# A relational graph network on one core: one gathered tile in 66, and two in 66 in the last layer, are loaded row by row from other queues than GpSimd's

## The reference

```python
h = relu(layernorm(x))
x = x + segment_sum((h * src_norm)[src], dst) * dst_norm      # layer 0
h = relu(layernorm(x))
for l in range(2):                                            # layers 1 and 2
    seg = dst * 65 + edge_type
    agg = segment_sum(h[src], seg)
    cnt = maximum(segment_sum(1, seg), 1)
    conv = relu(einsum('nrd,rdk->nk', agg / cnt, W[l]) + h @ root[l] + bias[l])
    h = conv + relu(h @ res_W[l] + res_b[l])
out = x + h
```

## Time and profile before

| | |
|---|---|
| median of 3 runs | 12882.89 us (12865.02 to 12885.59) |
| the profiled execution | 12863.82 us, its span 12861.9 us |
| POOL | busy 9338.7 us (73%) |
| PE | busy 5821.2 us (45%) |
| DVE | busy 5213.0 us (41%) |
| ACT | busy 1786.2 us (14%) |
| mean granted TensorE clock | 0.693 of 2.4 GHz |

### The profile page before, as it was taken

How to read it: one execution, slowest core, us unless ns; L and a number is a source line. 1 busy time by engine, 2 the same in 40 slices (tenths; PEclk the granted TensorE clock), 3 DMA queues, 4 the chain that set the end, 5 groups by cost and what they waited for, 6 DMA issues and landing times.

```text
span 12861.9 us, 134064 instructions
## 1 busy us (share of the span) xinstructions
PE 5821.2 (45%) x30566; PEld 4624.6 (36%) x30766; DVE 5213.0 (41%) x19303; ACT 1786.2 (14%) x4595; POOL 9338.7 (73%) x9756
## 2 busy tenths in 40 slices
PE   3544444444444445555555555554333333333333
PEld 3433333333333334333333333333333333333333
DVE  9866666666666642222222222222222222222222
ACT  5611111111111111111111111110000000000000
POOL 3277777777777767777777777776777777777776
PEclk6777777777777777777777777776666666666666
DMA  1244444444444442222222222222111111111112
GB/s 42 51 143 140 142 140 145 138 145 138 145 139 144 138 113 78 83 82 80 79 81 83 82 81 78 83 83 52 28 28 28 28 28 28 28 28 28 28 28 36
DMA packets 523546, 1050.43 MB, mean 82 GB/s; under 512 B 216706, under 2 KB 249232, under 8 KB 523280
## 3 DMA queue, kind: packets, MB, share of 16 engines
q1 hardware_dynamic: 212816, 729.64, 15.5%
q0 software_dynamic: 310464, 318.54, 13.2%
HBM read 600.17 MB, written 447.31 MB: 81 GB/s over the span
## 4 chain that ended last, share of the span: by engine, by line
POOL 69%; issue 26%; DVE 2%; DMA 1%; PE 1%; POOLq 1%; SPq 0%; DVEq 0%; ACT 0%; ACTq 0%
POOL rows L518 69%; DVE ystage L885 2%; DMA rows<-h_table,idx_st 1%; PE sums_ps L787 0%; POOLq L512 0%; POOLq L261 0%; DMA rows<-y_table,idx_st 0%; SPq L290 0%; DMA y_table<-ystage 0%; DVEq L879 0%; POOLq L260 0%; DMA h_table<-scr 0%; PE y_ps L738 0%; DVEq L885 0%; SPq L270 0%
## 5 line engine op out<-in xcount | busy, mean ns | idle before, releaser
L518 POOL DMA_INDIRECT rows<-y_table,idx_st x6468 | 6133.4, 948 | 2075.7 <-issue 2075.7
L787 PE MATMUL sums_ps<-onehot,rows 128*64 128x128 f32 (+1 forms) x19404 | 3896.8, 390 | 6487.1 <-DMA rows<-y_table,idx_st 4459.9
L787 PEld LDWEIGHTS sums_ps<-onehot,rows 128*64 128x64 f32 (+1 forms) x19404 | 3645.0, 211 | 6705.9 <-issue 5114.4
L518 POOL DMA_INDIRECT rows<-h_table,idx_st x3234 | 3083.7, 954 | 1010.3 <-issue 1005.7
L914 DVE TENSOR_SCALAR onehot<-iota,dst_rel,w_sb 128x128 f32<-128x128 bf16 x6468 | 1727.7, 361 | 3986.2 <-PE sums_ps L749 2276.9
L921 DVE TENSOR_SCALAR_CACHE_REDUCE w_raw<-scr,key_col 128x384 bf16<-128x384 f32 x3234 | 1744.6, 603 | 0.0
L738 PE MATMUL y_ps<-w_parts,hT 128*128 128x512 bf16 (+1 forms) x5200 | 1256.4, 375 | 194.0 <-ACT hT L614 161.0
L912 DVE TENSOR_SCALAR onehot<-iota,dst_rel 128x128 f32<-128x128 bf16 x3234 | 676.3, 300 | 1105.9 <-PE sums_ps L749 899.5
L601 ACT ACTIVATE idx_st<-pair_i 128x11 int32 (+1 forms) x594 | 125.9, 213 | 7162.6 <-PE sums_ps L787 4875.4
L622 ACT ACTIVATE ystage<-y_ps 128x512 f32<-128x512 f32 (+1 forms) x1800 | 1020.8, 567 | 517.8 <-PE y_ps L738 411.8
L984 DVE TENSOR_SCALAR rr<-rr 128x64 f32<-128x64 f32 x200 | 43.4, 217 | 2145.6 <-PE block_ps L759 2145.6
(11 more groups left out here) (125 smaller groups left out, 1759.1 us busy)
## 6 DMA issues: line engine op xcount, KB each, us to landing
y_table<-ystage SPq DMA_DIRECT2D x400, 768.0 KB, 3.6
scr<-key_row SPq DMA_DIRECT2D x297, 832.0 KB, 7.3
y_table<-ystage SPq DMA_DIRECT2D x200, 608.0 KB, 3.1
rows<-y_table,idx_st POOLq DMA_INDIRECT x6468, 2.4
rows<-h_table,idx_st POOLq DMA_INDIRECT x3234
rr<-y_table SPq DMA_DIRECT2D x200, 64.0 KB, 1.8
w_raw<-in_L_gnn_W SPq DMA_DIRECT2D x4, 1040.0 KB
h_table<-scr SPq DMA_DIRECT2D x1, 3200.0 KB, 17.0
```

The lines of the kernel that those rows point to most:

```text
L518: pool.indirect_dma_start(out=rows[:, j, k, 0:D], out_offset=None, in_=table, in_offset=bass.IndirectOffsetOnAxis(ap=idx_st[:, j, k:k + 1] ...
L787: ins = nc.tensor.matmul(sums_ps[u][0:width, c:c + P], rows[:, j, k, 0:width], onehot[:, (J * u + j) % 2, k, :], start=False, stop=False)
```

## The change

In every pair of steps the last tile of the last group, (u, j, k) = (1, 2, 10), is no longer gathered by POOL. SP loads its 128 rows with 128 DMAs of one row each, into a buffer of its own, `rows_sp`. For that it reads the row numbers into 32 registers at a time from a new table in HBM (`idx_row`), in four parts of 32 rows: parts 0 and 2 at the start of steps u = 0 and u = 1, parts 1 and 3 between the second and the third save. It may begin when PE is through with the pair before. In layer 2 the last tile of group (0, 2) goes the same way through ACT's queue into `rows_act`: parts 2 and 3 behind the staging at j = 1 of step 0, and parts 0 and 1 of the next pair behind the stagings at j = 1 and j = 2 of step 1. PE waits for these rows before the group that holds the tile. POOL's loop now has a body of two steps. The prologue gets two conversions on DVE, which make the row numbers, and two DMAs that save them.

```diff
+            for k in range(2):
+                sp.wait_ge(idx_ready, k + 1)
+                sp.dma_start(idx_row[k].rearrange("(c p) e -> p c e", p=P),
+                             i_row[k].rearrange("p (c e) -> p c e", e=P)).then_inc(idx_saved, 16)
...
+            def load_rows(l, i, part):
+                table = h0_table if l == 0 else y_table[l - 1]
+                tile_of = (i * 2 + 1) * T + T - 1
+                sp.load(row_regs, idx_row[min(l, 1)][bass.ds(tile_of, 1), part * PART:(part + 1) * PART])
+                for n, reg in enumerate(row_regs):
+                    e = part * PART + n
+                    at = sp.snap(reg, min_val=0, max_val=table.shape[0] - 1)
+                    sp.dma_start(rows_sp[e:e + 1, 0:D], table[bass.ds(at, 1), :])\
+                      .then_inc(row_loaded[l][part], 16)
...
                     with sp.Fori(0, S // 2) as i:
+                        wait_alone(sp, agg_done[l], i * 2 * J + J)
                         for u in range(2):
                             s = i * 2 + u
+                            load_rows(l, i, 2 * u)
...
                                 save_y(l, s, u, range(YG - 1))
+                            load_rows(l, i, 2 * u + 1)
...
-                            for k in range(K):
+                            for k in range(K - 1 if (u, j) == (1, J - 1) or (l, u, j) == (2, 0, J - 1) else K):
                                 pool.indirect_dma_start(
...
                                 stage(l, s + 1, j)
                                 if l < 2:
                                     emit_y(l, s, u, i, Y_AFTER[j])
+                                elif u == 0 and j == 1:
+                                    load_rows(i, 2)
+                                    load_rows(i, 3)
+                                elif u == 1:
+                                    load_rows(i + 1, j - 1)
...
+                                if (l, u, j) == (2, 0, J - 1):
+                                    for half in range(2):
+                                        pe.wait_ge(row_loaded_act[half], (i + 1) * (32 * PART))
+                                if (u, j) == (1, J - 1):
+                                    for part in range(4):
+                                        pe.wait_ge(row_loaded[l][part], (i + 1) * 16 * PART)
...
             dve.wait_ge(tr_done, TG)
+            dve.wait_ge(tr_done, 2 * TG)
+            dve.wait_ge(win_ready, 1)
+            V.tensor_scalar_min(i_row[0], f_src, float(NBK * P - 1)).then_inc(idx_ready, 1)
             step(V.tensor_scalar(f_src, f_src, float(NBK * P - 1), float(RX), ALU.min, ALU.mult))
             V.tensor_tensor(f_pair, f_src, f_pair, ALU.add).then_inc(f_ready["pair"], 1)
             dve.wait_ge(f_ready["pair"], 1)
+            V.tensor_copy(i_row[1], f_pair).then_inc(idx_ready, 1)
```

More of the change, by code:

```diff
@@ L82, in gnn_kernel @@
         key_row = nc.dram_tensor("key_row", [1 + ETP, P], f32, kind="Internal").ap()
+        idx_row = [nc.dram_tensor(f"idx_row{k}", [ETP, P], i32, kind="Internal").ap() for k in range(2)]
         dump = nc.dram_tensor("dump", [P, 2, 16], f32, kind="Internal").ap()
@@ L93, in gnn_kernel @@
         rows = sb("rows", [P, J, K, D + 1], f32)
+        rows_sp = sb("rows_sp", [P, D + 1], f32)
+        rows_act = sb("rows_act", [P, D], f32)
         onehot = sb("onehot", [P, 2, K, P], f32)
@@ L222, in gnn_kernel @@
         out_saved = sem("out_saved")
+        idx_ready = sem("idx_ready")
+        idx_saved = sem("idx_saved")
+        row_loaded = [[sem(f"row_loaded{l}{n}") for n in range(4)] for l in range(3)]
+        row_loaded_act = [sem(f"row_loaded_act{n}") for n in range(2)]
         gathered = [[sem(f"gathered{l}{j}") for j in range(J)] for l in range(3)]
@@ L241, in gnn_kernel @@
         N_CONST = 5
+        PART = 32
         HEAD = P - OFF % P
@@ L329, in all_y_saved @@
                     sp.wait_ge(y_saved[l][slot], 16 * ((n + 1 - slot) // 2 + 1))
+            row_regs = [sp.alloc_register(f"row{n}") for n in range(PART)]
+            def load_rows(l, i, part):
[7 more added lines that the diff above has]
+                      .then_inc(row_loaded[l][part], 16)
             sp.wait_ge(flag_ready, 1)
@@ L511, in _ @@
                             pool.wait_ge(y_saved[l - 1][slot], 16 * ((n + 1 - slot) // 2 + 1))
-                    with pool.Fori(0, S) as s:
-                        for j in range(J):
-                            q = s * J + j
+                    with pool.Fori(0, S // 2) as i:
+                        for u, j in [(u, j) for u in range(2) for j in range(J)]:
+                            q = i * 2 * J + u * J + j
                             wait_alone(pool, idx_staged[l], q + 1)
                             wait_alone(pool, agg_done[l], q + 1)
-                            for k in range(K):
+                            for k in range(K - 1 if (u, j) == (1, J - 1) or (l, u, j) == (2, 0, J - 1) else K):
                                 pool.indirect_dma_start(
@@ L623, in emit_y, with load_rows @@
                                              y_ps[c % 2][:, 0:y_cols(c)], ACT.Copy).then_inc(y_read[l], 1)
+            row_regs = [act.alloc_register(f"row{n}") for n in range(PART)]
+            def load_rows(i, part):
+                tile_of = i * (2 * T) + (T - 1)
+                act.load(row_regs, idx_row[1][bass.ds(tile_of, 1), part * PART:(part + 1) * PART])
+                for n, reg in enumerate(row_regs):
+                    e = part * PART + n
+                    at = act.snap(reg, min_val=0, max_val=NBK * P * RX - 1)
+                    act.dma_start(rows_act[e:e + 1, :], y_table[1][bass.ds(at, 1), :])\
+                       .then_inc(row_loaded_act[part // 2], 16)
             act.wait_ge(flag_ready, 1)
@@ L634, in _ @@
                         nc.scalar.activation(col[:, 3:4], eps[:, :], ACT.Copy).then_inc(y_read[l], 1)
+                    if l == 2:
+                        act.wait_ge(idx_saved, 32)
+                        for slot in range(2):
+                            wait_alone(act, y_saved[1][slot], 16 * ((YG * NBK + 1 - slot) // 2 + 1))
+                        load_rows(0, 0)
+                        load_rows(0, 1)
                     with act.Fori(0, S // 2) as i:
@@ L783, in _ @@
                                 pe.wait_ge(onehot_ready[l], q + 1)
-                                pe.wait_ge(gathered[l][j], (s + 1) * 16 * K)
+                                if j < J - 1:
+                                    pe.wait_ge(gathered[l][j], (s + 1) * 16 * K)
+                                elif l < 2:
+                                    pe.wait_ge(gathered[l][j], i * (16 * (2 * K - 1)) + 16 * (K + u * (K - 1)))
+                                else:
+                                    pe.wait_ge(gathered[l][j], (s + 1) * 16 * (K - 1))
+                                if (l, u, j) == (2, 0, J - 1):
[4 more added lines that the diff above has]
+                                        pe.wait_ge(row_loaded[l][part], (i + 1) * 16 * PART)
                                 for k in range(K):
                                     c = column_of(j * K + k, T)
-                                    ins = nc.tensor.matmul(sums_ps[u][0:width, c:c + P], rows[:, j, k, 0:width],
+                                    of = rows[:, j, k, 0:width]
+                                    if (u, j, k) == (1, J - 1, K - 1):
+                                        of = rows_sp[:, 0:width]
+                                    elif (l, u, j, k) == (2, 0, J - 1, K - 1):
+                                        of = rows_act[:, :]
+                                    ins = nc.tensor.matmul(sums_ps[u][0:width, c:c + P], of,
                                                            onehot[:, (J * u + j) % 2, k, :], start=False, stop=False)
```

12 lines of the change are left out of this document (11 added, 1 removed).

## The result

The changed kernel takes 14,903.64 us (median of 4 runs, 14,895.16 to 14,918.42), the kernel before 12,882.61 us on the same chip: ratio 1.1572, 95% interval 1.1554 to 1.1591. That is 2,021 us slower, where 180 us faster was forecast.

What follows compares the result with a forecast made beforehand. POOL was taken to bound the kernel. Gathers -245, ACT's wait +49, layer ends +12 and prologue +4 gave -180 us: 12,864 to 12,684 profiled, 12,703 us forecast with 19 us to the median; range 12,640 to 13,560.

Steps and rivals of the forecast that it cites:

- What bounds the kernel now: Whole kernel: POOL is never idle for want of work; each gather costs 1.25 us, so 196 fewer save 245 us.
- 6 at a layer's end: End of layers 0 and 1: PE starts the last group later, 6 us for each layer, 12 us in all.
- The price of one part: Loading 32 rows on a queue: 11.7 us for rows plus 1.7 for register loads, 13.4 us, bounds 10.6 and 38.
- the estimate of 13,800 us: Whole time by the skill's rule of some 200 ns per register: part 19.6 us, ACT's circle 103 us.
- p: Price of one part, 32 rows with their register loads, on SP's or ACT's queue: taken as 13.4 us.
- SP, layers 0 and 1: SP's queue: parts 0 to 2 lie in waiting time, part 3 is in time; nothing lost within these layers.
- ACT, layer 2: ACT's queue, where the change is tight: a deadline for POOL's buffer and ACT's own circle, 4p + 24 to 25 us.
- The forecast's 49 us: Layer 2: POOL waits 1.0 us for ACT's staging in each of 49 pairs.
- the deadline at p = 12.9: Layer 2: ACT's staging after (0, 2) reaches POOL's group (1, 2) in time, at 33.5 us, while p is below 12.9.
- Prologue: Before POOL's start: two more DVE passes of 1.89 us each and a 0.5 us wait, 4 us later.
- Register loads that grow with the number of registers: Rival: p = 17.7, ACT's circle 95.5 us in place of 80, 760 us lost; +540, 13,423 us; chance 0.29.
- the 19.5: Layers 0 and 1: SP's part 3 is in time for POOL's buffer at 33.5 us while p is below 19.5 us.

Runs made afterwards that it cites:

- c3: Changed kernel with row numbers loaded into registers once a layer, all row DMAs kept (same 32 rows copied): 12,665.44 us against 12,869.1 for the kernel before.
- h_half: Changed kernel without ACT's tile and with only parts 0 and 2 of SP's tile loaded: 12,708.26 us against 12,883.51 for the kernel before.
- v_three: Changed kernel without ACT's tile; SP loads parts 1 to 3, POOL gathers the other 32 rows: 12,933.91 us against 12,869.1 for the kernel before.
- y_early: Changed kernel without ACT's tile, next pair's first register load moved ahead of the last save's wait: 22,465.79 and 22,176.77 us, only on chips with kernel before at 15,000 to 15,100.
- b3: Changed kernel with ACT's tile of layer 2 alone, SP loading no rows: 13,345.73 us, ratio 1.0368 to the kernel before.
- p_pad: Kernel before with four blocks of long-fulfilled waits (96 instructions each) added in SP's loops: 12,885.88 us, ratio 1.0003 to the kernel before.
- w2_layer2: Second run of the changed kernel with SP's tile in layer 2 only, none on ACT; chip with kernel before at 15,000 to 15,100 us: 17,486.43 us, ratio 1.1654.
- a2_sp_alone: Second run of the changed kernel without ACT's tile, on a chip where the kernel before takes 15,000 to 15,100 us: 22,544.63 us, ratio 1.4953.
- d: Changed kernel, all register loads kept, one of each part's 32 rows fetched; chip with kernel before at 15,000 to 15,100 us: 15,167.59 us, ratio 1.0109.
- b: Changed kernel with ACT's tile alone, SP loading no rows; chip with kernel before at 15,000 to 15,100 us: 17,234.03 us, ratio 1.1486.
- w: First run of the changed kernel with SP's tile in layer 2 only, none on ACT; chip with kernel before at 15,000 to 15,100 us: 17,395.54 us, ratio 1.1516.
- c: Changed kernel with registers loaded once a layer, all row DMAs kept; chip with kernel before at 15,000 to 15,100 us: 20,682.47 us, ratio 1.3785.
- a: First run of the changed kernel without ACT's tile, on a chip where the kernel before takes 15,000 to 15,100 us: 22,587.32 us, ratio 1.5054.

## Why the prediction was wrong

**What bounds the kernel now: right.** In c3 and h_half, where the queues are in time, POOL's pace sets each layer and gives back 47 to 55 us for 49 gathers, and 105 for 98 (forecast 61 and 122, less 6 at a layer's end).

**The price of one part: the step that failed.** "A load of one register takes 0.727 us. I take that for each, since the instruction is the same": 1.7 us for both loads. The rows of the changed kernel in layer 1:

```profile
L350 SPq TENSOR_LOAD <-idx_row_ptr x196: 1012/1088/1437, 5754.0 to 10293.6; - x196
...
L350 SPq TENSOR_LOAD <-idx_row x196: 3490/3654/4136, 5755.3 to 10294.8; - x196
```

The load of 32 numbers takes 3.65 us, 0.11 a register; the address 1.09; with the operations between, 5.2 us. That lies within the stated bounds of 1.0 and 23 us, but is three times the value taken. The Trainium skill (Runtime: NRT & Kernel Launch, Instruction fetch mechanics) gives some 200 ns a register even in bulk: right that the price grows with the registers, about twice too dear here; the estimate of 13,800 us made from it was nearer than the forecast. The row's price was 13.4 us for 32 on SP and 12.1 on ACT, for 11.7: on SP a row is 0.22 us for the DMA, 0.03 for the move, 0.04 for the register operation and 0.12 us of gaps between them, of which the prediction had counted 0.04. p came to 18.7 and 17.3 us in place of 13.4. With the rows as measured and loads of 1.7 us it would be 15.1 on SP, whose circle would be 78.7 us and hidden, and 13.8 on ACT, near what was forecast: by this arithmetic, which no run tested, the loads' size alone turned the sign. c3 shows it for loads of nothing.

**SP, layers 0 and 1: the second step that failed.** "Parts 0 to 2 lie in time that SP spends waiting" and "It is in time while p is below 19.5 us". At 18.7 that still says no loss, and 1,553 of the 2,040 us are lost there. The step followed one part to one deadline and took for granted that SP reaches it idle, its second save done 6.6 us behind PE's (1, 1). In the pair shown PE is through with (1, 1) at 8048.61, and the two saves end at 8068.41: 19.8 us behind it, because part 2, late behind part 1, held the queue until 8066.35. PE starts (1, 2) 39.7 us behind, where 8.4 + p would be 27.1, and is through with it 44.4 us behind; POOL wanted the buffer at 33.5. The prediction never went once around SP's queue, as it did for ACT's. The circle, 18.3 + 4p, passes 82.6 us at p = 16.1. Two terms of the 18.3 were not in it: the wait of 8.9 us behind the last part, and the jump, 4.2 us, which SP's short body does not have before. v_three agrees in layer 1: three parts are 18.3 + 56.1 = 74.4 us, under 82.6, and nothing is lost. I did not measure the wait's place in the circle by itself; y_early was to do it.

**Layer 0** loses twice what layer 1 does. There the address load takes 3.63 us in the median, for 1.09 in layer 1, so p is 3.6 + 3.7 + 0.2 + 13.6 = 21.1 and the circle 18.3 + 84.4 = 102.7 us. POOL's loop turns take 104.2 us on average, 11.9 more than in layer 1, which makes up the 571 us between the two layers' losses. The row in layer 0, and the loads of parts 2 and 3 of one pair with that of the next pair's part 0:

```profile
L350 SPq TENSOR_LOAD <-idx_row_ptr x196: 1042/3630/5341, 577.8 to 5681.7; - x196
L350 SPq TENSOR_LOAD <-idx_row_ptr x3: 1155/2897/3524, 3049.8 to 3107.8; - x3
```

The 3.52 and 2.90 us are the loads of parts 2 and 3, which SP issues straight behind loads of keys and saves; the 1.16 us is part 0's, behind the jump. It is so in the whole layer: the address load takes 1.2 us in the median for part 0, whose last load of keys was issued 13 us before, and 4.7, 3.6 and 4.5 us for parts 1, 2 and 3, 1.1 to 1.8 us behind one. In layer 1, with saves and no keys ahead of parts 1 and 3, it takes 1.09. h_half has the same tables and loads of keys, but issued 13 and 16 us before its parts, and its address loads are short, but for the first:

```profile
L350 SPq TENSOR_LOAD <-idx_row_ptr x98: 1006/1050/5286, 577.9 to 4557.3; - x98
```

So what the dear loads have in common is a load of keys issued just before, and not the length of the loop body, which is the same for all four parts. No run moved the keys, so that they are the cause is argued and not shown. In v_three three parts at 21.1 us would give 81.6 us, and it takes 83.9: in layer 0 the sum is not exact.

**ACT, layer 2: right mechanism, price mis-sized.** With long parts "its circle bounds that layer": the chain has 19% on ACT's queue, and PE waits for rows_act 49 times. At p = 17.3 the circle 4p + 24.7 is 93.9 us; POOL's loop turns in layer 2 of b3 take 91.8. The forecast's 49 us were not that circle, which at a p of 13.4 is 78.3 us and under 80, but the deadline at p = 12.9: at the measured price ACT went past both.

**Prologue: right.** POOL's first loop starts 3.7 (c3) to 5.7 us (v_three) later, 4 were forecast.

**The rivals.** "Register loads that grow with the number of registers", p = 17.7, chance 0.29, was the true one in its mechanism. Its layer 2 is 760 less 122 us for the gathers, 638 us more; b3 has 473. That its whole time, 13,423 us, lies near b3's 13,346 is luck, since it counts 196 removed gathers and b3 has 49. It missed 1,481 us because it used the 19.5 for SP too.

## What to carry to other kernels

Price a queue's work by walking once around its loop: every issue, register load, wait and the jump, against the pace it must keep; a deadline check for one transfer is not enough. Count what fetches the addresses beside the DMAs: here 32 rows took 13.4 us and their two register loads 5.2, and the 5.2 decided. Measure one bulk load before building on it. When two experiments contradict each other, look at what the unchanged kernel takes on their chip before looking at the theories.

## What the runs showed of the hardware

- A gather over 32 partitions costs POOL 0.867 us, one over 128 0.944 (v_three).
- With a loop body grown by 384 instructions SP stands still behind each jump back, 3.8 us in the median of layers 0 and 1 and 2.4 in layer 2 (p_pad), for 0.1 to 0.2 us in the kernel before; the added instructions, fulfilled waits, take 0.028 us each.
- A load of 32 registers takes 3.65 us, one of an address 1.09, and the latter 3.6 to 4.7 us in the median where loads of keys and saves were issued just before it.
- On the chips where the kernel before takes 15,000 to 15,100 us, POOL's gathers keep 0.944 us and 0.30 of issue, but ACT and DVE stand still and are released by what the trace calls remote, a semaphore without a releaser on record. w2_layer2's waits, whose layers 0 and 1 are those of the kernel before:

```profile
ACT idx_st L639 <- remote: 8840.7, 578, 58.0
PEld sums_ps L850 <- issue: 5415.0, 655, 89.6
DVE onehot L981 <- remote: 4782.8, 280, 25.0
POOL rows L556 <- ACT idx_st L639: 4700.3, 504, 60.9
PE sums_ps L850 <- DMA rows_sp<-y_table: 4195.4, 49, 89.4
```

The kernel before shows no such wait where it takes 12,883 us; where it takes 15,000 it has no trace. A row's move and DMA on SP there take up to 1.4 us (a2_sp_alone):

```profile
L354 SPq MOVE rows_sp<-y_table x12544: 1/29/1424, 8286.3 to 22504.8; - x200
L354 SPq DMA_DIRECT2D rows_sp<-y_table x12544: 1/221/1453, 8286.4 to 22504.8; - x200
```

and a burst of 32 rows, 13.4 us elsewhere and at times here, takes 40.21 and 41.62 us at 12006.11 and 12054.04. The loss grows with the issues in SP's and ACT's bodies (d 1.01, b and w 1.15, c 1.38, a 1.50) and is small where only the register loads stay (d), which fits a late supply of instructions. That is argued only, and c, which issues more than a, speaks against the body alone. The kernel with the padded body, which would have told, did not run on such a chip.
